# First attention of a two-layer block: score queries of two heads packed into one moving operand, and keys laid out by 0/1 columns

## The reference

```python
# layer 0, 16 heads of 16 features, Lkv = 154
xq  = ada_ln(x, cond, Wss_q);  xkv = ada_ln(ctx, cond, Wss_kv)
q   = (xq @ Wq + bq).reshape(B, Lq, 16, 16)
k,v = split((xkv @ Wkv + bkv).reshape(B, Lkv, 2, 16, 16))
attn = softmax(einsum('bqhd,bkhd->bhqk', q, k) / 4)
x   = x + einsum('bhqk,bkhd->bqhd', attn, v).reshape(B, Lq, 256) @ Wp + bp
```

## Time and profile before

| | |
|---|---|
| median of 3 runs | 496.98 us |
| the profiled execution | 496.63 us |
| its span in the trace | 494.8 us |
| set-up, until keys(0, 0) | about 46 us |
| 16 groups of the first attention | about 46 to 234 us |
| between the layers | 234 to 261 us |
| second layer | 261 to 494.8 us |
| mean granted PE clock | 0.976 |

### The profile page before, as it was taken

The page is one execution under the profiler, slowest core; times in us unless marked ns, Lnnn a source line. Parts: engine busy times, 40 slices in busy tenths (PEclk is TensorE's granted clock), DMA queues, the critical chain, the costliest instruction groups (busy, mean ns, idle before and its releaser), DMA issues.

```text
span 494.8 us, 6881 instructions
## 1 busy us (share of the span) xinstructions
PE 458.3 (93%) x2418; PEld 358.3 (72%) x2418; DVE 321.9 (65%) x797; ACT 193.0 (39%) x331; POOL 138.5 (28%) x208
## 2 busy tenths in 40 slices
PE   3966989998999999999979999999999999999994
PEld 3644666766777667666447898888888888888883
DVE  4778766467647745756867558875687657842345
ACT  4921433444343434345442344422444334432210
POOL 2074055205200400200004322354233533315333
PEclk9977999999999999999988999999999999999998
DMA  8801002600010011000011000001000010001001
GB/s 292 316 0 44 1 19 69 228 7 23 21 44 1 1 43 44 1 0 1 1 38 32 0 2 1 1 1 43 1 0 1 3 42 1 1 2 42 1 1 42
DMA packets 7314, 17.45 MB, mean 35 GB/s; under 512 B 880, under 2 KB 2288, under 8 KB 7152
## 3 DMA queue, kind: packets, MB, share of 16 engines
q1 hardware_dynamic: 5040, 11.57, 6.7%
q10 hardware_dynamic: 1584, 3.15, 1.7%
q0 software_dynamic: 656, 2.29, 1.7%
HBM read 14.45 MB, written 2.10 MB: 33 GB/s over the span
## 4 chain that ended last, share of the span: by engine, by line
PE 80%; DVE 8%; ACT 4%; issue 3%; POOL 2%; DMA 1%; ACTq 1%; POOLq 0%; DVEq 0%
PE bank L1124 53%; PE pair L1124 14%; PE pair L1217 4%; PE bank L1259 3%; PE bank L1256 2%; DVE lnt L791 2%; ACT keys L612 2%; DVE nm L908 1%; PE bank L1225 1%; PE bank L1269 1%; DVE keys L869 1%; PE bank L1280 1%; DMA small_sb<-in_small 1%; ACTq L591 1%; DVE vtail L888 1%
## 5 line engine op out<-in xcount | busy, mean ns | idle before, releaser
L578 POOL TENSOR_TENSOR hs<-hid,hs 128x512 fp32r<-128x512 f32 x48 | 64.6, 1346 | 125.5 <-DVE hs L1077 125.5
L1124 PE MATMUL bank<-nx,w1h 128*128 128x512 f32 x224 | 74.7, 415 | 0.0
L1124 PE MATMUL pair<-w2h,hs 128*128 128x256 f32 x384 | 70.2, 281 | 0.0
L736 ACT ACTIVATE hid<-bank,ab 128x512 f32<-128x512 f32 x48 | 33.1, 689 | 88.3 <-PE bank L1124 88.2
L1124 PEld LDWEIGHTS pair<-w2h,hs 128*128 128x128 f32 x384 | 62.4, 189 | 4.3 <-POOL hs L578 0.2
L908 DVE TENSOR_REDUCE nm<-pair 128x4 fp32r<-128x616 f32 x64 | 51.1, 799 | 20.2 <-PE pair L1217 19.6
L665 ACT ACTIVATE pt<-bank 128x512 f32<-128x512 f32 x80 | 47.3, 599 | 29.1 <-PE bank L1124 27.1
L1077 DVE CAST hs<-hid 128x512 fp32r<-128x512 f32 x48 | 20.5, 428 | 58.3 <-ACT hid L736 57.5
L1124 PE MATMUL pair<-w2l,hs 128*128 128x256 f32 x192 | 54.1, 282 | 0.0
L1124 PE MATMUL bank<-nx,w1l 128*128 128x512 f32 x112 | 44.5, 398 | 0.0
L1124 PEld LDWEIGHTS bank<-nx,w1h 128*128 128x128 f32 x224 | 39.9, 191 | 6.2
(11 more groups left out here) (191 smaller groups left out, 914.6 us busy)
## 6 DMA issues: line engine op xcount, KB each, us to landing
stage<-in_w1n POOLq DMA_DIRECT2D x7, 256.0 KB, 3.3
w1e_sb<-in_w1e SPq DMA_DIRECT2D x1, 1792.0 KB, 7.5
x_sb<-in_x SPq DMA_DIRECT2D x3, 512.0 KB, 14.3
stage<-in_w1a SPq DMA_DIRECT2D x3, 512.0 KB, 6.5
stage<-in_ew2T SPq DMA_DIRECT2D x3, 512.0 KB, 3.9
out_x<-x_sb SPq DMA_DIRECT2D x3, 512.0 KB, 2.7
wss_sb<-in_wss SPq DMA_DIRECT2D x2, 512.0 KB, 8.6
x_sb<-in_x ACTq DMA_DIRECT2D x1, 512.0 KB, 5.0
```

Source lines behind the costliest of these rows:

```text
L578: g_.tensor_tensor(hs[:, q % 3, 1, :], hid[:, q % 2, :], hs[:, q % 3, 0, :], ALU.subtract).then_inc(hl_r, 1)
L736: A(dst, B_H[n % 2][:, :], ACT.Silu, bias=ab1[:, m, c // CPB:c // CPB + 1]).then_inc(h_r, 1)
L1124: ins = mm(dst, a, b_, start=first and i == 0, stop=last and i == len(terms) - 1, skip_group_check=free)
```

## The change

- The 64 upper or lower partitions of a pair of heads now carry the rest of the query: tile xq has two versions s = 0, 1. In version 0 partitions 0 to 63 (heads 0, 1) hold rounded queries and partitions 64 to 127 hold the rest of the same two heads; version 1 is the mirror. So a block of 128 keys takes one product (kk, xq) in place of two; the tail block takes two (one for each version).
- ACT writes the rounded queries with two instructions of 64 partitions in place of one of 128; DVE the rest likewise. keys(g, 0) waits for the first half, keys(g, 2) for the second.
- The combined keys kc are built with two versions too; tiles kr (for rows), kk and kt are made from it by a product with a 0/1 column over all 128 partitions: kr and kt by DVE (place), kk by ACT (blocks). The clearing of keys on ACT and POOL's kb are gone; POOL clears pads of kc and half of each xq. The table small is 90 columns in place of 69.
- lnt holds 4 row tiles in place of 2 (and the use of stage1 for two of them is gone), and the steps rsqrt and norm of the next chunk's layer norm stand earlier in the list.

```diff
+PAIR = ((slice(0, 64), slice(64, 128)), (slice(64, 128), slice(0, 64)))
...
-        KAW, KBW = GH * LK + P, GH * P + P
-        keys_ = sb("keys", (P, B, NG, KAW + KBW), F32R, l0)
-        ka, kb = keys_[:, :, :, 0:KAW], keys_[:, :, :, KAW:KAW + KBW]
+        KRW, KKW = GH * LK, GH * P
+        keys_ = sb("keys", (P, B, NG, KRW + KKW + 2 * P), F32R, l0)
+        kr, kk = keys_[:, :, :, 0:KRW], keys_[:, :, :, KRW:KRW + KKW]
+        kt = keys_[:, :, :, KRW + KKW:KRW + KKW + 2 * P].rearrange("p b g (s n) -> p b g s n", s=2)
...
+                        fill[1] += (("rsqrt", c + 1),)
+                        fill[4] += (("norm", c + 1, 0),)
+                        fill[5] += (("norm", c + 1, 1),)
-                        fill[0] += (("xt", c + 1, 0), ("norm", c + 1, 1))
+                        fill[0] += (("xt", c + 1, 0),)
...
+            g_.memset(kc[:, :, :, :, LK:KP].bitcast(F32), 0.0).then_inc(kc_0, 1)
-            pool.wait_ge(kh_r, NG)
-            pool.wait_ge(keys_0, B * NG)
-            for j in range(GH):
-                r = slice(32 * j, 32 * j + 32)
-                for dst, o, w in ((P * j, 0, P), (P * GH + 32 * j, P, KT)):
-                    g_.tensor_scalar(kb[r, :, :, dst:dst + w].rearrange("p b g n -> p g b n"), kh[r, :, :, o:o + w],
-                                     small[r, SM["m0"][0]:SM["m0"][1]], small[r, SM["m16"][0]:SM["m16"][1]],
-                                     ALU.mult, ALU.add).then_inc(kb_r, 1)
-                    pool.wait_ge(kb_r, 2 * j + (1 if w == P else 2))
+            pool.wait_ge(ss_mm, 2)
+            g_.memset(xq[GH * 16:P, :, 0, :].bitcast(F32), 0.0).then_inc(xq_0, 1)
+            pool.wait_ge(xq_0, 1)
+            g_.memset(xq[0:GH * 16, :, 1, :].bitcast(F32), 0.0).then_inc(xq_0, 1)
+            pool.wait_ge(xq_0, 2)
...
-            def clear(b):
-
-                act.wait_ge(zero_r, 1)
-                for g in range(NG):
-                    A(keys_[:, b, g, :], zero[:].broadcast_to([P, KAW + KBW]), ACT.Copy).then_inc(keys_0, 1)
-
-            clear(0)
...
-            clear(1)
...
                 act.wait_ge(k_mm, gi + 1)
-                A(kg[:, gi], K_BANK[gi][:, 0:B * KP].rearrange("p (b n) -> p b n", b=B)[:, :, 0:LK], ACT.Identity,
-                  bias=bkm[:, gi:gi + 1], scale=sm("m1")).then_inc(kg1_r, 1)
-                A(kh[:, gi], K_BANK[gi][:, 0:B * KP].rearrange("p (b n) -> p b n", b=B), ACT.Identity,
-                  bias=sm("bk", gi)).then_inc(kh_r, 1)
+                k4 = K_BANK[gi][:, 0:B * KP].rearrange("p (b n) -> p b n", b=B)[:, :, 0:LK]
+                if gi >= 2:
+                    act.wait_ge(kg_r, gi - 1)
+                A(klo[:, gi % 2], k4, ACT.Identity, bias=sm("bkl", gi), scale=sm("m1")).then_inc(kg1_r, 1)
+                for s_, (r, low) in enumerate(PAIR):
+                    A(kc[low, gi, s_, :, 0:LK], k4[r], ACT.Identity, bias=small[r, SM["bkh"][0] + gi:SM["bkh"][0] + gi + 1],
+                      scale=small[r, SM["m0"][0]:SM["m0"][1]]).then_inc(kh_r, 1)
...
+            def blocks(b):
+
+                act.wait_ge(kc_0, 1)
+                act.wait_ge(kg_r, NG)
+                for j in range(GH):
+                    A(kk[:, b, :, P * j:P * j + P], kc[:, :, j // 2, b, 0:P], ACT.Copy, scale=sm("mkey", j % 2)).then_inc(kk_r, 1)
+
+            blocks(0)
...
-                A(qh[:, g % 2, :], B_P[g % 2][:, :], ACT.Identity, bias=sm("bq", g % NG)).then_inc(qh_r, 1)
+                for s_, (r, low) in enumerate(PAIR):
+                    A(xq[r, g % 2, s_, :], B_P[g % 2][r, :], ACT.Identity,
+                      bias=small[r, SM["bq"][0] + g % NG:SM["bq"][0] + g % NG + 1]).then_inc(qh_r, 1)
...
-                dve.wait_ge(kh_r, gi + 1)
+                dve.wait_ge(kh_r, 2 * gi + 2)
...
+                for s_, (r, low) in enumerate(PAIR):
+                    ins = V.scalar_tensor_tensor(kc[r, gi, s_, :, 0:LK], k4[r], small[r, SM["bk"][0] + gi:SM["bk"][0] + gi + 1],
+                                                 klo[r, gi % 2], ALU.add, ALU.subtract)
+                ins.then_inc(kg_r, 1)
...
             def place(b):
 
                 for j in range(GH):
-                    r = slice(32 * j, 32 * j + 32)
-                    for dst, o, w in ((LK * j, 0, LK), (LK * GH + 32 * j, P, KT)):
-                        ins = V.tensor_copy(ka[r, b, :, dst:dst + w], kg[r, :, b, o:o + w])
-                ins.then_inc(ka_r, 1)
+                    ins = V.tensor_scalar(kr[:, b, :, LK * j:LK * j + LK], kc[:, :, j // 2, b, 0:LK], sm("mrow", j), None, ALU.mult)
+                ins.then_inc(kr_r, 1)
+                for s_ in range(2):
+                    ins = V.tensor_tensor(kt[:, b, :, s_, :].rearrange("p g (j n) -> p g j n", j=GH),
+                                          kc[:, :, s_, b, P:KP].unsqueeze(2).broadcast_to([P, NG, GH, 32]),
+                                          sm("mtail", GH * s_, GH).unsqueeze(1).unsqueeze(3).broadcast_to([P, NG, GH, 32]), ALU.mult)
+                ins.then_inc(kt_r, 1)
...
             def shift(g):
 
                 dve.wait_ge(nm_d, g + 1)
-                dve.wait_ge(qh_r, g + 1)
+                dve.wait_ge(qh_r, 2 * g + 2)
                 if g >= 2:
                     dve.wait_ge(st_d, (GH + 1) * (g - 1))
-                V.scalar_tensor_tensor(ql[:, g % 2, :], B_P[g % 2][:, :], sm("bq", g % NG), qh[:, g % 2, :],
-                                       ALU.add, ALU.subtract).then_inc(ql_r, 1)
+                for s_, (r, low) in enumerate(PAIR):
+                    V.scalar_tensor_tensor(xq[low, g % 2, s_, :], B_P[g % 2][r, :],
+                                           small[r, SM["bq"][0] + g % NG:SM["bq"][0] + g % NG + 1], xq[r, g % 2, s_, :],
+                                           ALU.add, ALU.subtract).then_inc(ql_r, 1)
...
-                    ins = mm(B_S[s][:, 0:2 * LK], qh[:, g % 2, P * q:P * q + P],
-                             ka[:, c // CPB, gi, 2 * LK * s:2 * LK * (s + 1)], start=True, stop=True)
+                    ins = mm(B_S[s][:, 0:2 * LK], xq[:, g % 2, s, P * q:P * q + P],
+                             kr[:, c // CPB, gi, 2 * LK * s:2 * LK * (s + 1)], start=True, stop=True)
...
-                if k == 0:
-                    pe.wait_ge(ql_r, g + 1)
+                if k == 0 and g % (NC * NG // B) == 0:
+                    pe.wait_ge(kk_r, GH * (b + 1))
+                if k in (0, 2):
+                    pe.wait_ge(ql_r, 2 * g + 1 + k // 2)
                 if n == 0:
-                    pe.wait_ge(kb_r, 2 * GH)
                     pe.wait_ge(v_r, 2 * B)
                 if n >= 2:
                     pe.wait_ge(ex_d, n - 1)
                 if k < GH:
-                    a, b_ = ka[:, b, gi, LK * k:LK * k + P], kb[:, b, gi, P * k:P * k + P]
+                    terms = [(kk[:, b, gi, P * k:P * k + P], xq[:, g % 2, k // 2, :])]
                 else:
-                    a, b_ = ka[:, b, gi, LK * GH:LK * GH + P], kb[:, b, gi, P * GH:P * GH + P]
-                passes(B_ST[n % 2][:, :], [(a, qh[:, g % 2, :]), (b_, ql[:, g % 2, :])]).then_inc(st_d, 1)
+                    if g % (NC * NG // B) == 0:
+                        pe.wait_ge(kt_r, b + 1)
+                    terms = [(kt[:, b, gi, s, :], xq[:, g % 2, s, :]) for s in range(2)]
+                passes(B_ST[n % 2][:, :], terms).then_inc(st_d, 1)
```

92 lines of the change are left out of this document (43 added, 49 removed).

## The result

The changed kernel takes **493.61 us** (median of 20 runs, 491.47 to 496.86). The kernel before takes 496.44 beside it (20 runs, 494.5 to 499.27). The ratio is 0.9947, 95% interval 0.9928 to 0.9966: faster, by 2.8 us (0.5%) and not by 14.3. The forecast of 482.7 is missed, and so is its range (475.5 to 491). A profile shows one execution, and not always a typical one: that of the changed kernel took 496.52 us, 2.9 above its median, at a mean granted clock of 0.969, the low end of the 20 (0.969 to 0.984); that of the kernel before took 496.63. So I read groups from the traces, and totals from the medians.

A forecast was written before the change was run, and what follows sets the result against it. The prediction took PE's instruction stream (busy 93% of the span) to set the time. Its terms, 8.3 + 4.0 + 2.0 = 14.3 us, came off the profiled 496.63 us; with 0.35 for the median, 482.7 us, range 475.5 to 491.

The forecast's parts named there:

- term 1: First attention, 16 groups: one product per key block in place of two, less waits from halved query writes, gains 8.3 us.
- layer norm moves: Next chunk's layer norm made earlier: 1.5 us each in g6 and g10, 1.0 in g2, sum 4.0 us.
- set-up, and what is left: Before and in g0: clearing gone, vtail faster, ACT copies added; 2.0 us kept behind g0.
- POOL beside DVE: Set-up: POOL's additions and w1 pieces move beside DVE's splits, perhaps up to five times as long; only in the lower bound.
- the walk through g13: Typical group, time by time: ACT's second half loses 0.2 us, DVE's 0.3; 0.6 of 0.92 us is kept.
- rival B: DVE paces the groups: its 0.74 us comes out in each, leaving 0.18; 6.7 us gained, 490.3 us; chance 0.18.
- Rival C: Slower: both halves on ACT and DVE delay PE in each group, +0.51 us times 16, 505.2 us; chance 0.04.
- D: Rival: block products were covered by PE's waits for exp, other edits cancel; 0 us gained, 497.0 us; chance 0.04.

The follow-up runs named there:

- x_drop_halves: The kernel before without the second product of key blocks 0 to 3, with rounded query and rest each written by two 64-partition instructions: 497.11 us, ratio 1.0011.
- a_ln: The changed kernel with the steps rsqrt and norm of the next chunk's layer norm back at their old places: 496.88 us, ratio 1.0020.
- a_pool: The changed kernel with POOL's additions of bp and first w1 piece held back until DVE has written the first key versions: 491.02 us, ratio 0.9897.
- x_drop: The kernel before without the second product of key blocks 0 to 3, nothing added or moved: 489.95 us, ratio 0.9894.
- a_order: The changed kernel with the second key block put ahead of the first rows step in every group: 492.74 us, ratio 0.9935.
- a_pool_order: The changed kernel with the edits of a_pool and a_order together: 490.81 us, ratio 0.9887.
- a_pad: The changed kernel with the products of key blocks 0 to 3 issued twice in groups g3, g6 and g7 only: 494.36 us, ratio 0.9957.
- a_dup: The changed kernel with each product of key blocks 0 to 3 issued twice in all groups: 496.42 us, ratio 1.0015.

## Why the prediction was wrong

The terms side by side:

| term | predicted | measured | by |
|---|---|---|---|
| 1. one product per block, halved queries | -8.3 | +0.8 | x_drop_halves |
| 2. layer norm moves | -4.0 | -3.3 | a_ln |
| 3. set-up, and what is left | -2.0 | -0.3 | remainder of -2.8 |
| of 3: POOL beside DVE | 0 (in the lower bound only) | +2.6 | a_pool |

The remainder also holds what the packing itself does, which wasn't run apart, and all that the terms do to one another; without the 2.6 us it would be -2.9. It flatters the set-up: by the traces the first vtail comes 1.2 us later than before, and 1.1 us of gain lies behind the last group, where nothing was forecast.

**What bounds the kernel.** Right as a share, wrong as a price. With PE busy in 10.70 of 10.70 us I took each removed start distance of 0.23 us as won unless a wait ate it. Under that 100% stood chains a few tenths of a microsecond behind PE: exp, z, m_ev, reductions. x_drop alone gives 6.4 of 14.7 us, and 2.6 of 7.4 in g8 to g15 where the clock is at 1.00.

**The failed step** is in term 1, in the walk through g13, where "0.29 rows" follows the first block without a wait, and in the words against rival B: "version 1 is needed two blocks later only". That holds for the keys steps, and for DVE's rest. But rows(n, 0) is the *second* step of a group and takes, of the query written just before, both versions: the weight load waits 0.45 us for ACT there, and 6.1 us in nine such places. The step needed was to ask for each reader of a tile, and not only for the one that the edit names. This wait is a sign of the error and not its whole price: a_order and a_pool_order cut it to 4.2 us and gained 0.9 and 0.2 us. The price is that of the second halves on ACT and on DVE together, 7.2 us in x_drop_halves where the walk had 5.1, beside removed products that are worth 6.4 us and not 14.7. The walk's second part failed with it: rows 2 was to start 0.12 us sooner after keys(g, 0) than before and starts 0.02 later (3.67 for 3.65); rows 3 0.46 sooner and starts 0.16 sooner. And keys(g13, 0) itself starts 3.35 us after the vtail of g12, where it was 3.20. The bounds of the term, 0.2 to 0.92 us a group, were wrong at the lower end: "all of DVE's 0.74 us comes out" left out ACT's 0.69. Rival C had the sum of both (0.69 + 0.74 - 0.92 = +0.51 a group); over 16 groups it is ten times what x_drop_halves lost, but in g14 it is near the 0.42 measured.

**Rival B** (490.3) came nearest, by a hair: it is 3.3 us off and D (497.0) 3.4. B had the right kind of cause, a second half that comes out in each group, but on DVE alone; ACT's costs about as much.

**Layer norm.** POOL was done at 115.69 and not near 113.8, and the first lnt pair stands in front of the rest of the query as foreseen:

```profile
115.72 2.02 DVE L790 TENSOR_SCALAR lnt<-x_sb,mv,rs 128x256 f32<-128x256 f32 x2
...
117.78 1.53 DVE L920 SCALAR_TENSOR_TENSOR xq<-bank,small_sb,xq 64x512 fp32r<-64x512 f32 x2
```

From its first keys product to that of g7, g6 lasts 12.93 us (15.20 before), less than the 13.5 to 14 given. The wait of PE at the transposes in g2 stayed almost whole, 1.37 for 1.47 us, as the prep tile does hold their bank; g2 was shorter all the same.

**Set-up.** vtail took 1.03 us, as predicted. rows(0, 0) came at 35.67 and not 32.6. The price had been named (POOL's additions "move beside the splits") and then put into the bound alone, as something that might happen; nothing in the order kept the two apart. POOL makes 1.05 us of these 3.1 (a_pool). Most of the rest is ACT: from its first K copy to the table load it takes 9.4 us (19.18 to 28.58) where it took 5.65 (20.53 to 26.18), so the extra copies cost 3.7 us and not 2.3. From rows(0, 0) to keys(0, 0) the stretch shrank by 4.4 us (10.44 for 14.85), near the 5.0 that the prediction implies. keys(0, 0) came at 46.11 (46.05 before), where 3.6 us earlier was forecast.

The first exp came at 49.57 and not at 46.0. Its product was out at 46.58, but ACT had the second batch's four key blocks (2.56 us) ahead of it, and they began only behind the query halves:

```profile
46.11 0.47 PE L1128 MATMUL bank<-xq,keys 128*128 128x512 f32 x1 [0.58 <-DVE xq L920]
46.83 1.89 DVE L866 TENSOR_SCALAR keys<-kc,small_sb 128x616 fp32r<-128x616 f32 x4
46.98 2.56 ACT L640 ACTIVATE keys<-kc,small_sb 128x512 fp32r<-128x512 f32 x4
...
49.57 1.09 ACT L663 ACTIVATE pt<-bank 128x512 f32<-128x512 f32 x2
50.31 0.47 PE L1128 MATMUL bank<-xq,keys 128*128 128x512 f32 x1 [1.44 <-ACT pt L663]
```

The prediction had counted these 2.4 us, and the exp follows keys(0, 0) by 3.46 us, near the 3.7 that it gave; it is late because keys(0, 0) is. PE waits 1.44 us for the exp.

**The clock** had no term. In g3 the granted clock is 0.88 in the changed kernel and in a_pool, where it is 1.00 before; a_pad and a_dup, with g3's products doubled, keep 1.00 and take 1.2 us less for the group. From 84 to 94 us, before and then after:

```profile
84.00:94.00 10.00, 10.00 (x63) 7.47 (x62) 4.50 (x7) 3.25 (x6) 2.88 (x4) 1.00 0.71 262
...
84.00:94.00 10.00, 9.81 (x53) 7.99 (x54) 4.01 (x6) 2.90 (x5) 2.59 (x3) 0.83 0.74 267
```

This fall takes more than the 0.9 us that the prediction had for g3, and the group got longer (14.16 for 12.56 us). In the profiled execution the granted clock is at 0.71 from 127.3 to 140.5 us and at 0.89 after it, where it is 1.00 before the change:

```profile
114.50:127.30 12.80, 11.42 (x68) 7.40 (x67) 11.82 (x19) 6.83 (x13) 8.79 (x14) 1.00 0.08 22
127.30:140.50 13.20, 13.20 (x65) 11.01 (x68) 4.90 (x10) 4.88 (x8) 0.00 (x0) 0.71 0.12 30
140.50:152.00 11.50, 11.38 (x54) 7.42 (x47) 6.11 (x10) 5.16 (x9) 0.00 (x0) 0.89 0.10 36
```

In the stretch before the fall PE was busy 11.42 of 12.80 us at 2.4 GHz. a_pool, with g6 as thin (10.14 of 11.50), shows no fall there and 11.21 us for g7, and the kernel before is as thin too (11.36 of 13.00) and shows none. So this execution's fall is no constant of the kernel, and why it comes in one execution and not in another stays open. Over the 20 runs of the changed kernel the time follows the mean granted clock (correlation -0.96), from 491.47 us at 0.981 to 496.86 at 0.969.

## What to carry to other kernels

An engine that is busy for 100% of a stretch can still be no faster than the chains beside it: before a removed instruction is counted at its start distance, list for each engine how close behind it the next wait is, and expect only a part where there are several (here less than half). An instruction of half the partitions costs a whole one, so splitting a write doubles it, and its price must be asked at every reader of the tile, above all at the first one in program order. When an edit moves POOL work, look at what DVE does in the new place; a wait that keeps the two apart gave 2.6 us here, nearly as much as the whole change. And read from the executions' clocks whether the profiled one is typical before you explain a group by it.

## What the runs showed of the hardware

- Half the partitions cost the same time: ACT 0.69 us for 128 x 512 and 1.39 for two of 64 x 512, DVE 0.74 and 1.53.
- Half the columns cost less: the reduction takes 0.799 us for 616 columns and 0.477 for 308, so by these two 1.05 ns a column and about 0.15 us besides.
- Four products of 128 x 616 with a column take 1.89 us on DVE, 0.47 each (line 866 above), less than the 0.55 that I took. The Trainium skill, VectorE: DVE Perf Modes, section "Mode 2×_2P — use both read ports for one tensor", let me estimate 0.4 to 0.5, and the trace agrees.
- DVE's copy of 128 x 512 took 1.65 us beside POOL and 0.43 without. POOL's four additions took 2.96 us in the meeting and 2.77 in a_pool, its copy w1h 1.06 and 0.61. Over the meeting DVE's four operations lose 3.0 us and POOL's six 0.7: DVE pays most.
- The granted clock goes between its two levels within a group: g3 took 14.1 us with a mean granted clock of 0.88 and 13.0 at 1.00.
